# Last mixture of experts: finished rows scattered to the output, a table of its own zeroed from the GpSimd queue in the first loop, weight copies on ScalarE

## The reference, cut to what matters

```python
logits = xf @ router_w + router_b
vals, idx = jax.lax.top_k(logits, TOPK)
scores = jax.nn.softmax(vals, axis=-1)
cap = int(np.floor(n * CAP_FRAC))
oh = jax.nn.one_hot(idx, E, dtype=jnp.float32)
pos = jnp.cumsum(jnp.cumsum(oh, axis=0), axis=1).astype(jnp.int32)
emask = oh * (pos < cap)
tmask = jnp.sum(emask, axis=-1)
assign = jnp.einsum('tke,e->tk', emask, jnp.arange(E, dtype=jnp.float32)).astype(jnp.int32)
m = jnp.max(assign, axis=-1)
def ff(w1e, w2e, w3e):
    h = jax.nn.gelu(xf @ w2e * (xf @ w1e), approximate=False)
    return h @ w3e
y = y_all[m, jnp.arange(n)]
slot = jnp.where(tmask[..., None] > 0, y[:, None, :], xf[:, None, :])
out = jnp.einsum('tkD,tk->tD', slot, scores)
```

## Time and profile before

| | us |
|---|---|
| median of 3 runs (lowest, highest) | 1675.45 (1674.0, 1679.46) |
| the profiled execution's own time | 1675.38 |
| its span, first to last instruction | 1673.6 |
| PE busy | 1423.6 (85%) |
| DVE busy | 966.6 (58%) |
| ACT busy | 749.0 (45%) |
| POOL busy | 232.3 (14%) |
| mean granted TensorE clock | 0.922 of full speed |

### The profile page before, as it was taken

One profiled execution on the slowest core, in us unless ns is written; L12 is line 12 of the kernel. 1 busy time (PEld: TensorE's weight loads), 2 busy tenths in 40 slices (PEclk: granted clock), 3 DMA queues, 4 the chain that ended last, 5 costly groups with the idle time before them and its releaser, 6 DMA issues.

```text
span 1673.6 us, 43831 instructions
## 1 busy us (share of the span) xinstructions
PE 1423.6 (85%) x17681; PEld 878.2 (52%) x17681; DVE 966.6 (58%) x2541; ACT 749.0 (45%) x1927; POOL 232.3 (14%) x201
## 2 busy tenths in 40 slices
PE   4889888696499999999958999889989898999672
PEld 3343434393266666766633466346644564456462
DVE  4354635323477777777723676576665776477532
ACT  1323142251266666666613276327723672447431
POOL 1011120123030030200010200030002100120124
PEclk7989999797799999999978899999989998899897
DMA  9600000023230100100021000000000000000012
GB/s 327 264 17 1 17 1 7 17 58 98 77 140 4 26 19 10 35 4 16 4 76 43 1 2 2 5 7 2 2 5 7 2 2 1 7 1 1 6 55 70
DMA packets 62072, 60.07 MB, mean 36 GB/s; under 512 B 27952, under 2 KB 47024, under 8 KB 60720
## 3 DMA queue, kind: packets, MB, share of 16 engines
q1 hardware_dynamic: 59536, 53.04, 10.0%
q0 software_dynamic: 2048, 4.20, 0.9%
q10 hardware_dynamic: 288, 0.03, 0.0%
HBM read 32.73 MB, written 24.51 MB: 34 GB/s over the span
## 4 chain that ended last, share of the span: by engine, by line
PE 69%; DVE 15%; issue 4%; SPq 4%; DMA 3%; ACT 3%; POOL 2%; ACTq 0%; POOLq 0%; DVEq 0%
PE ps L1126 7%; PE ps L1514 6%; PE ps L1533 5%; PE ps L500 5%; PE ps L1547 4%; PE ps L1106 4%; PE ps L1116 4%; DVE arena L586 4%; PE ps L1147 4%; PE ps L258 4%; PE ps L1502 3%; PE ps L474 3%; PE ps L1161 2%; PE ps L1556 2%; PE ps L797 2%
## 5 line engine op out<-in xcount | busy, mean ns | idle before, releaser
L1259 DVE TENSOR_REDUCE nmax<-ps 128x1 f32<-128x512 f32 x256 | 166.8, 683 | 56.3 <-PE ps L1116 55.7
L1590 ACT ACTIVATE arena<-ps,arena 128x512 f32<-128x512 f32 (+3 forms) x256 | 135.5, 531 | 119.1 <-DVE arena L1650 112.9
L1650 DVE TENSOR_REDUCE arena<-ps 128x1 f32<-128x512 f32 (+3 forms) x256 | 124.3, 487 | 78.8 <-PE ps L1518 76.7
L1219 ACT ACTIVATE arena<-ps,nmax 128x512 f32<-128x512 f32 x172 | 119.0, 692 | 80.8 <-DVE nmax L1259 79.3
L1533 PE MATMUL ps<-sqc,arena 128*128 128x128 f32 x640 | 106.6, 287 | 20.0 <-DVE arena L1658 19.7
L586 DVE TENSOR_REDUCE arena<-ps 128x8 f32<-128x1232 f32 x64 | 89.2, 1438 | 40.3 <-PE ps L462 40.1
L258 PE MATMUL ps<-identb 128*128 128x512 bf16 x408 | 110.0, 430 | 1.4 <-DVE kcol L707 1.4
L1267 DVE COPY arena<-ps 128x512 f32<-128x512 f32 x128 | 88.0, 688 | 39.9 <-PE ps L1126 38.4
L1514 PE MATMUL ps<-arena 64*128 64x384 f32 (+3 forms) x512 | 106.2, 493 | 0.0
L1658 DVE TENSOR_SCALAR arena<-arena 128x512 f32<-128x512 f32 (+3 forms) x256 | 100.8, 394 | 9.1
L598 DVE RECIPROCAL arena<-ps 128x128 f32<-128x128 f32 x8 | 7.7, 959 | 160.4 <-PE ps L500 160.4
(11 more groups left out here) (350 smaller groups left out, 2713.1 us busy)
## 6 DMA issues: line engine op xcount, KB each, us to landing
xs_d<-onehot SPq DMA_DIRECT2D x3, 3072.0 KB, 29.6
cw<-in_cw SPq DMA_DIRECT2D x2, 2048.0 KB, 13.4
rv<-in_rv SPq DMA_DIRECT2D x2, 1536.0 KB, 19.7
late<-in_gw SPq DMA_DIRECT2D x3, 1024.0 KB, 10.8
arena<-xs_d SPq DMA_DIRECT2D x46, 64.0 KB, 1.8
xs_d<-arena SPq DMA_DIRECT2D x46, 64.0 KB, 1.6
xs_d<-onehot SPq DMA_DIRECT2D x1, 2560.0 KB, 22.4
onehot<-q_s SPq DMA_DIRECT2D x96, 8.0 KB
```

The source lines that it names most:

```text
L1219: nc.scalar.activation(PB[k % 6], ps[:, k % 5, :], ACT.Exp, bias=nmax[:, u:u + 1], accum_out=rsum[:, b % 2, u:u + 1]).then_inc(SD["exp"], 1)
L1259: nc.vector.tensor_reduce(nmax[:, k % NU:k % NU + 1], ps[:, k % 5, :], AX.X, ALU.max, negate=True)\
L1590: nc.scalar.activation(TF["p%d" % (n % 2)][:, h * S:h * S + wd], ps[:, FSB[n % 2][h], 0:wd], ACT.Exp, bias=TF["nmax"][:, k4:k4 + 1], accum ...
L1650: nc.vector.tensor_reduce(TF["nmax"][:, k4:k4 + 1], ps[:, FSB[n % 2][h], 0:wd], AX.X, ALU.max, negate=True)\
```

## The change

- **A table of its own for G.** `gs_d` has 17536 rows of 258 floats: the normed token, `rest` (128 floats each), `cy` and the token's number less 4096. The three parts of a row are kept side by side in SBUF (`G4`, in the space of C's weights), and `pool_G_send` scatters whole rows of 1032 bytes. Rows that no token owns are zero, so that their number plus 4096 lies outside the output.
- **Zeros.** `pool_G_zero` fills `gs_d` with four plain DMAs from the POOL queue, in the first loop before `pool_X` of `b` = 0. REGION falls from 2560 to 2176 rows, so `xs_d` has 20480 rows in place of 23552, and SP's four fills become 10 x 512 floats per partition each.
- **Finished rows.** In the G loop DVE computes `cy * y + rest` from the loaded tile in place of the plain copy, POOL adds 4096 to the tokens' numbers and scatters the 128 rows to the output with one indirect DMA, which skips the rows outside it. Gone are the 23 stores to `xs_d`, the 16 gathers, the 16 DVE operations and the four output DMAs. The load of tile s + 6 now waits for the result and the numbers of tile s instead of its transpose.
- **Weights.** ACT copies the weights in place of POOL, into three buffers, two tiles ahead.
- **Masks.** The mask preparation goes from DVE to POOL (`pool_prepare`), ahead of the zeros; a short rest of it stays on DVE, now after the norm of B. Three small DVE operations ahead of the E loop make the tokens' numbers.

```diff
-REGION = 2560
+REGION = 17 * P
+GROWS = E1 * REGION + P
@@ dve_A
             if b:
                 dve_C_choose(dve, ch, b - 1)
-            else:
-                dve_prepare(dve)
             dve_X_values(dve, b, "B")
@@ dve_X
             if k == "B" and b == 0:
+                dve_prepare(dve)
                 dve_masks(dve)
...
+        def pool_prepare(pool):
+            pool.wait_ge(s_const[1], 16 * len(GROUPS[1]))
+            nc.gpsimd.tensor_copy(xmask[:, :, 0:KP], xmask_in)
+            nc.gpsimd.tensor_copy(xmask[:, :, KP:KW], xmask_in[:, :, 0:KW - KP])
+            for mask, given in ((amask, amask_in), (kmask, kmask_in)):
+                nc.gpsimd.memset(mask[:, :, KS:KP], MASKED)
+                nc.gpsimd.tensor_scalar(mask[:, :, 0:KS], given[:, :, :], MASKED, None, ALU.mult)
+                ins = nc.gpsimd.tensor_scalar(mask[:, :, KP:KW], given[:, :, 0:KW - KP], MASKED, None, ALU.mult)
+            ins.then_inc(s_mask, 1)
...
         def pool_G_send(pool, b):
             pool.wait_ge(SG["slot"], b + 1)
-            for n in range(NT):
-                nc.gpsimd.indirect_dma_start(xs_d, bass.IndirectOffsetOnAxis(ap=slot4[:, b * NT + n:b * NT + n + 1], axis=0),
-                                             yn4(b)[:, n, :], None).then_inc(SC["sent"], 16)
+            if b == 0:
+                pool.wait_ge(SG["zero"], 16 * 4)
+            for n in range(b * NT, b * NT + NT):
+                nc.gpsimd.indirect_dma_start(gs_d, bass.IndirectOffsetOnAxis(ap=slot4[:, n:n + 1], axis=0),
+                                             G4[:, n, :], None).then_inc(SC["sent"], 16)
@@ act_G
+            def weights(s):
+                e = act.value_load(expert4[0:1, s:s + 1], min_val=0, max_val=E2 - 1)
+                if s >= 3:
+                    act.wait_ge(SC["h"], NS + s - 2)
+                nc.scalar.copy(TG[f"w{s % 3}"].rearrange("p (m n) -> p m n", m=2),
+                               gw12[:, :, bass.ds(e, 1), :].rearrange("p m o n -> p m (o n)")).then_inc(SC["w1"], 1)
+
+            act.wait_ge(SG["table"], 1)
+            weights(0)
+            weights(1)
             linear(0)
             for s in range(NS):
+                if s + 2 < NS:
+                    weights(s + 2)
                 act.wait_ge(SG["p"], s + 1)
@@ dve_G
-                    dve.wait_ge(SC_st[s % 4], 16 * (st_c[s % 4] + s // 4))
-                V.tensor_copy(TG[f"y{s % 4}"], ps[:, 6 + s % 2, 0:P]).then_inc(SC["yb"], 1)
-            for b in range(B):
-                dve.wait_ge(SC_yg[b], 2 * 16 * NT)
...
+                    dve.wait_ge(SG_out[s % 4], 16 * (s // 4))
+                V.scalar_tensor_tensor(TG[f"y{s % 4}"], ps[:, 6 + s % 2, 0:P], XBG[s % NXB][:, 2 * P:2 * P + 1],
+                                       XBG[s % NXB][:, P:2 * P], ALU.mult, ALU.add).then_inc(SC["yb"], 1)
@@ sp_G
-                sp.wait_ge(SC["yb"], NS + s + 1)
-                sp.dma_start(xs_d[bass.ds(r, P), :], TG[f"y{s % 4}"]).then_inc(SC_st[s % 4], 16)
...
+                if s >= NXB:
+                    sp.wait_ge(SC["yb"], NS + s - NXB + 1)
+                    sp.wait_ge(SG["idx"], s - NXB + 1)
+                sp.dma_start(XBG[s % NXB], gs_d[bass.ds(r, P), :]).then_inc(SC_ld[s % NXB], 16)
+            for z in range(4):
+                sp.wait_ge(SG_out[z], 16 * st_c[z])
+
+        def pool_G_zero(pool):
+            zero = onehot[:, :, :].rearrange("p i n -> p (i n)")[:, 0:GW4]
+            pool.wait_ge(s_zero, 1)
+            rows = gs_d.rearrange("(p r) d -> p r d", p=P)
+            for z in range(4):
+                r0, r1 = z * (GROWS // P) // 4, (z + 1) * (GROWS // P) // 4
+                nc.gpsimd.dma_start(rows[:, r0:r1, :], zero.unsqueeze(1).to_broadcast([P, r1 - r0, GW4])).then_inc(SG["zero"], 16)
@@ pool_G
+            for s in range(NS):
+                pool.wait_ge(SC_ld[s % NXB], 16 * (ld_c[s % NXB] + s // NXB + 1))
+                if s >= 4:
+                    pool.wait_ge(SG_out[s % 4], 16 * (s // 4))
+                nc.gpsimd.tensor_scalar(gidx[:, s % 4:s % 4 + 1], XBG[s % NXB][:, 2 * P + 1:GW4], 2.0 * B * S, None, ALU.add)\
+                    .then_inc(SG["idx"], 1)
+                pool.wait_ge(SG["idx"], s + 1)
+                pool.wait_ge(SC["yb"], NS + s + 1)
+                nc.gpsimd.indirect_dma_start(out_rows, bass.IndirectOffsetOnAxis(ap=gidx[:, s % 4:s % 4 + 1], axis=0),
+                                             TG[f"y{s % 4}"], None, bounds_check=B * S - 1, oob_is_err=False)\
+                    .then_inc(SG_out[s % 4], 16)
```

More of the change, by code:

```diff
@@ L863, in dve_C @@
             dve.wait_ge(SC["count"], 1)
[L864 removed]
+            dve_tiles(ch, SC["table"], XROWS - P)
             dve.wait_ge(SC["table"], 1)
@@ L1686, in pool_F @@
                     .then_inc(SF["qr"], 1)
-        SG = {n: sem("s_g_" + n) for n in ("gate", "d", "e2", "oh", "cum", "seen", "pick", "rank", "slot", "count", "table", "a", "p")}
+        SG = {n: sem("s_g_" + n) for n in ("gate", "d", "e2", "oh", "cum", "seen", "pick", "rank", "slot", "count", "table", "a", "p", "zero", "idx")}
+        SG_out = [sem("s_g_out%d" % i) for i in range(4)]
         ld_c, st_c = ([len(range(z, NS, n)) for z in range(n)] for n in (NXB, 4))
@@ L1695, in decoder @@
         used[0] = 0
[L1696 to L1697 removed]
+        GW4 = 2 * P + 2
+        G4 = cw[:, 0:NTT * GW4].rearrange("p (t n) -> p t n", n=GW4)
+        XBG = [cut(GW4) for _ in range(NXB)]
+        g_p = sb("g_p", [P, 1])
+        gidx = sb("g_idx", [P, 4], mybir.dt.int32)
+        gs_d = nc.dram_tensor("gs_d", (GROWS, GW4), F32, kind="Internal").ap()
+        out_rows = out.rearrange("b s d -> (b s) d")
+        TG = dict(**{f"xT{z}": cut(P) for z in range(2)}, **{f"w{z}": cut(2 * HID2) for z in range(3)},
                   **{n + str(z): cut(HID2) for n in "aph" for z in range(2)}, **{f"y{z}": cut(P) for z in range(4)})
         TG.update(oh=sb("g_oh", [P, NT * 2 * E2])[:, :], cum=sb("g_cum", [P, NT * 2 * E2])[:, :], sum=sb("g_sum", [P, 2 * E2])[:, :])
[L1700 to L1702 removed]
+        yn4, xo4 = (lambda b, k=k: G4[:, b * NT:(b + 1) * NT, k * P:(k + 1) * P] for k in range(2))
+        cy4 = lambda b: G4[:, b * NT:(b + 1) * NT, 2 * P]
         gw12 = late[:, sum(LATE[:4]):sum(LATE[:6])].rearrange("p (m e n) -> p m e n", m=2, e=E2)
@@ L1895, in dve_G @@
             dve.wait_ge(SG["count"], 1)
-            dve_tiles(ch, SG["table"])
+            dve_tiles(ch, SG["table"], GROWS - P)
             def copy(s):
@@ L1932, in sp_G @@
             sp.wait_ge(SG["table"], 1)
-            def load(s):
-                r = sp.value_load(rows4[0:1, s:s + 1], min_val=0, max_val=XROWS - P)
+            for s in range(NS):
+                r = sp.value_load(rows4[0:1, s:s + 1], min_val=0, max_val=GROWS - P)
                 if s >= NXB:
-                    sp.wait_ge(SC["tx"], NS + s - NXB + 1)
-                sp.dma_start(XBG[s % NXB], xs_d[bass.ds(r, P), :]).then_inc(SC_ld[s % NXB], 16)
-            for s in range(NXB):
-                load(s)
@@ L2045, in _ @@
             sp_G(sp)
-            for b in range(B):
-                sp.wait_ge(s_xout, b + 1)
-                sp.dma_start(out[b:b + 1].rearrange("o (t p) d -> p (o t) d", p=P), xo4(b)).then_inc(s_store, 16)
-            sp.wait_ge(s_store, B * 16)
         @block.tensor
@@ L2135, in _ @@
             ch.turn(0)
+            ch(nc.vector.tensor_reduce(g_p[:, 0:1], c["tri"], AX.X, ALU.add))
+            ch(nc.vector.tensor_scalar(g_p[:, 0:1], g_p[:, 0:1], -1.0, float(P - 2 * B * S), ALU.mult, ALU.add))
+            ch(nc.vector.tensor_scalar(G4[:, :, 2 * P + 1], row["index"][:, 0:NTT], float(P), g_p[:, 0:1], ALU.mult, ALU.add))
             for b in range(B):
```

71 lines of the change are left out of this document (22 added, 49 removed).

## The result

The changed kernel takes 1728.9 us (median of 4 runs, 1725.2 to 1733.5), the kernel before 1674.7 beside it: a ratio of 1.0325, 95% interval 1.0286 to 1.0363. It is **slower by 54 us**; 1656.0 was forecast, within 1638 to 1690. The profiled execution took 1733.5, its span is 1731.7 against 1673.6: +58.1. That is the sum of a first loop 75.9 us later and a last mixture 17.5 us shorter; all the rest together is 0.3 shorter.

The account below looks back on a forecast made before the run. It took the closing gathers, SP's pace in the G loop and DVE's mask preparation at the start to bound the kernel. 1673.6 - 24.3 - 4.4 + 1.3 + 8 = 1654.2, with 1.8 us 1656.0; range 1638 to 1690.

Parts of the forecast that it names:

- the fills of `gs_d`: First loop: POOL's four fills delay keys of `b` = 0 and x of `b` = 1; +8 us including the masks' -5.2.
- The hold on POOL: Before the keys of `b` = 0: four fills at 8 us in issue, 32 us, keys at 58.5, 10.4 late.
- the upper bound of 7.5 ns a piece: POOL's fills: each piece costs what an indirect DMA's row does; 131.8 us, keys at 158, PE 110 us late.
- The upper bound for x (+17.5): x of `b` = 1: all 33.8 MB drained first, at 113, and 3 us to land.
- End of G, -24.3: Kernel's end: last copy, store, gathers and output DMAs, 28.2 us, become last operation and one scatter, 3.9 us.
- Pace of the G loop, -4.4: G loop: ACT's sequence sets 1.9 us a tile in place of 2.11, 0.21 saved on each of 21 tiles.
- The lower bound from the quickest pair of tiles, 1.52: G loop: PE's quickest pair of tiles starts 1.52 us apart, which would give -12.4 us.
- Masks: Start of `b` = 0: without mask preparation DVE's way from L338 to L390 falls from 6.8 to 1.6 us, -5.2.
- Larger rows and small operations: G's larger tile loads +0.4 and three small DVE operations ahead of E +0.9; together +1.3 us.
- A: Rival, first loop: fills cost nothing, POOL's hold ends before 46 us, x is in time; 1642.8 us, chance 0.20.
- B: Rival, scores of `b` = 0: POOL writes descriptors one by one, first loop stands still; 1675.4 to 1753 us, chance 0.16.
- C: Rival, G loop: no quicker, ACT fully in series at 2.33 us, +4.6 in place of -4.4; 1665.0 us, chance 0.12.

Follow-up runs that it names:

- keys on time: The changed kernel with its `gs_d` fills cut as 4 x 30 rows ahead of POOL's keys of `b` = 0 and 17 rows behind them: 1703.4 us, ratio 1.0175.
- late fills: The changed kernel with its four `gs_d` fills issued later, one behind `pool_X` of `b` = 1, one in `b` = 2, two in `b` = 3: 1645.5 us, ratio 0.9823.
- all four in `b` = 1: The changed kernel with all four fills of 1032-byte pieces issued one behind the other in `b` = 1, behind its keys and values: 1669.1 us (one run).
- numbers on DVE: The kernel with fills issued late, and in the G loop DVE computes the row numbers so that POOL issues scatters only: 1646.2 us, ratio 0.9839.

## Why the prediction was wrong

The step that failed is **the fills of `gs_d`**. It gave +8 us for the first loop with the masks' gain in it; it is +75.9. Inside it:

- *The hold on POOL.* I took 8 us for each of the four, like SP's fills, and put the keys at 58.5. Three took 1.86 us (0.43 ns a piece), the fourth 87. Neither an even hold nor the upper bound of 7.5 ns a piece was of the right form: writing the descriptors costs little until they no longer fit, and then the wait is as long as everything ahead takes to drain. Rule and trace had met in the sentence that I left beside the sum: by the Trainium skill (SBUF — State Buffer, the size table) an estimate of 1024 pieces per engine fit, and the fourth fill waits. The traces agree: 960 went in, 1096 did not, and 560 with the same bytes did. I used it for support of 32 us; with my own rate the three fills ahead, 13.5 MB at half of 385 GB/s, drain in 70 us, and the keys would have stood near 100, not 58.5. What no row of before showed is that the wait ends only when the last of the earlier fills has landed.
- *The drain.* I let all 33.8 MB pass at 385 GB/s. With pieces of 1032 bytes it was 292 and 260, and x of `b` = 1 was used at 145 (keys on time) and not at 110. This costs 58 us where it stands alone (keys on time), and I had 11.5. In the changed kernel it is hidden behind the hold, which it also lengthens: the hold lasts as long as the drain of the three fills. The row for 385 was of 2048-byte pieces from SP, and I changed the piece and the queue under it.
- The upper bound for x (+17.5) rested on the same rate and so was none.

**End of G, -24.3: right kind, too large**; -16.7 came (28.2 to 11.5). The last operation's start to the end is not 3.9 us, for two reasons: POOL is two scatters behind, so that the last one starts 4.3 us after DVE's last result does and not 0.65, since its pace was said to be "below any pace that the loop can have" and is the slowest of all engines, 2.12 (the 0.79 idle before each scatter was left out); and the end follows the start of the last scatter by 6.4 to 7.2 us in place of 3.2.

**Pace of the G loop, -4.4: wrong engine.** ACT, on which the sum was built, does not bound it: it is busy 25.6 of the 40.2 us of 20 tiles, PE 35.6. `hidden` follows `hidden` at 2.00 to 2.01 whether POOL has the numbers or not, and POOL's scatters at 2.12. `hidden` of tile 2 starts 12.5 us behind the last send, 11.5 before; whether the larger rows do that no run shows. DVE's last result comes 56.2 us behind the last send in place of 57.0: -0.8. The lower bound from the quickest pair of tiles, 1.52, was a pair beside a slow one.

**Masks: right**, and worth more than said, by the clock. **Larger rows and small operations**: not separated; within 1 us.

**The rivals.** A (fills cost nothing) names what late fills give, 1645.5 against its 1642.8, but its condition was not met, and the sum agrees by luck: it has -27.4 for G, where the trace of late fills has -18.0, and 6.9 us of spread between the loops make up for most of that. B had the outcome, the place (the scores of `b` = 0, waiting for POOL's keys) and the sign, with the wrong mechanism: descriptors are not slow to write. The break-even, a delay of 27.4 us, was passed by far: PE waited 75.2. C did not happen. B's chance of 0.16 was too small, as its condition, a hold over 54 us, could also be met by the full scratch, which I had worked out and not priced.

## What to carry to other kernels

Before a DMA that POOL writes itself is put ahead of work on POOL, count its pieces per DMA engine together with all that are still under way: here 960 went in at some 0.4 ns a piece, and at 1096 the queue stood until the last fill ahead had landed. Count its drain by the piece too, and put fills into the stretch in which the DMA engines are idle, behind and not ahead of the next load in their queue. Where two delays overlap, as the keys and x do here, price each as if it stood alone, with the rate of a row that has the same piece and the same queue; removing one uncovers the other.

## What the hardware showed unexpectedly

- A direct DMA from POOL with 272 pieces per engine is issued in 1.86 us; a fill of 4.5 MB with none ahead of it then lands in 39.7, 25.9 or 18.2 us with pieces of 516, 1032 or 2048 bytes.
- Waiting for room ended when the last earlier DMA had landed (landings at 117.8, 127.4, 124.5 and 280.7 us, starts at 118.1, 127.7, 125.0 and 281.1), not when there would be room for the new one. In the fifth case (all four in `b` = 1) the landing isn't recorded, but the wait is as long as three drains.
- POOL needs 1.79 us to turn 616 integers a partition into bf16 (L718); DVE took 0.64 and 0.45 for the two of them.
- With the fills all in `b` = 1 DVE's two products of 0.47 us took 10.16, and ended at 185.7, as POOL's L2194, L620 and L623 did at 185.4; DVE seems to have stood for POOL's operations; that this is the cause no run tested:

```profile
175.57 10.16 DVE L389 TENSOR_SCALAR arena<-tmp,dec_col 128x128 f32<-128x128 f32 x2
```

- From the start of the last scatter to the end of the span 6.4 to 7.2 us pass, while a gather took 2.33 us to land and the scatters 2.1 to 4.3 (numbers on DVE). What fills the rest stays open.
